# A Mamba block and a quantised feed-forward on one core: layer-norm statistics moved from VectorE to ScalarE, three more products per chunk on VectorE, pieces placed anew, and the last tile in column groups

## The reference, cut to what matters

```python
h = _layernorm(x) * (1 + ca) + sa
xc, z = split(h @ W_in.T, 2)                    # 1024 channels each
xc = silu(conv4(xc)); dlt, Bm, Cm = split(xc @ W_xproj.T)
delta = softplus(dlt @ W_dt.T + b_dt)
for t: state = exp(delta[t]*A) * state + delta[t]*xc[t]*Bm[t]     # 1024 x 16 states
       y[t] = sum_n state[:, n] * Cm[t, n]
x = x + ga * (((y + xc * D) * silu(z)) @ W_out.T)
h = _layernorm(x) * (1 + cb) + sb
g = silu(q(h) @ q(w_gate).T) * (q(h) @ q(w_up).T)     # 1408 wide, q: blocks of 16 to 4 bits
x = x + gb * (q(g) @ q(w_down).T)
```

## Time and profile before

| | |
|---|---|
| median of three runs | 5463.88 us (5456.84 to 5471.98) |
| the profiled execution | 5463.87 us, its span 5462.1 us |
| PE busy | 4869.5 us (89%) |
| DVE busy | 4934.1 us (90%) |
| POOL busy | 3984.4 us (73%) |
| ACT busy | 3061.0 us (56%) |

### The profile page before, as it was taken

The page is one execution under the profiler, slowest core; times in us unless marked ns, Lnnn a source line. Parts: engine busy times, 40 slices in busy tenths (PEclk is TensorE's granted clock), DMA queues, the critical chain, the costliest instruction groups (busy, mean ns, idle before and its releaser), DMA issues. The chain is left out here.

```text
span 5462.1 us, 76768 instructions
## 1 busy us (share of the span) xinstructions
PE 4869.5 (89%) x21996; PEld 3349.7 (61%) x21996; DVE 4934.1 (90%) x4312; ACT 3061.0 (56%) x6567; POOL 3984.4 (73%) x1960
## 2 busy tenths in 40 slices
PE   7589898898988989889898898976899999999999
PEld 3355555555555555555555555554788888888887
DVE  7899999999999999999999999999788888888887
ACT  2677777777777777777777777775211111111111
POOL 5899999999999999999999999999122222222221
PEclk9799999999999999999999999987999999999999
DMA  6455555555555555555555555555110101010100
GB/s 221 153 181 175 186 177 184 185 174 186 179 180 187 174 185 175 184 186 170 187 174 184 190 173 187 172 171 175 63 35 29 35 29 35 29 35 29 35 29 27
DMA packets 399478, 745.62 MB, mean 137 GB/s; under 512 B 44067, under 2 KB 44195, under 8 KB 398982
## 3 DMA queue, kind: packets, MB, share of 16 engines
q1 hardware_dynamic: 394758, 724.18, 40.5%
q0 software_dynamic: 4352, 17.30, 0.9%
HBM read 698.05 MB, written 43.26 MB: 136 GB/s over the span
## 5 line engine op out<-in xcount | busy, mean ns | idle before, releaser
L664 POOL TENSOR_TENSOR slot<-du,b_row 128x1024 f32<-128x1024 f32 x1024 | 2402.2, 2371 | 36.3 <-PE y_ps L1158 36.1
L1027 DVE TENSOR_TENSOR_SCAN decays<-decays,state,slot 128x1024 f32<-128x1024 f32 x608 | 1428.0, 2349 | 68.9 <-ACT slot L881 68.2
L872 ACT ACTIVATE decays<-delta,rate 128x512 f32<-128x512 f32 x2048 | 1327.0, 680 | 24.5 <-ACT state L859 2.8
L1158 PEld LDWEIGHTS y_ps<-ident,slot 128*128 128x128 f32 x8192 | 998.5, 148 | 322.9 <-issue 264.2
L1158 PE MATMUL y_ps<-ident,slot 128*128 128x128 f32 x8192 | 1088.8, 284 | 69.7 <-POOL slot L671 37.4
L1083 PE MATMUL work_ps<-h_t,win 128*128 128x512 f32 x2048 | 982.2, 624 | 114.7 <-ACT zs L750 92.4
L1512 POOL TENSOR_TENSOR hq<-hid,qinv 128x1408 f32<-128x1408 f32 x64 | 165.9, 2592 | 1227.2 <-DVE qinv L1538 1227.2
L671 POOL TENSOR_TENSOR slot<-slot,c_row 128x1024 f32<-128x1024 f32 x416 | 986.3, 2371 | 57.3 <-ACT state L859 57.3
L1027 DVE TENSOR_TENSOR_SCAN slot<-decays,state,slot 128x1024 f32<-128x1024 f32 x416 | 974.3, 2342 | 49.2 <-ACT slot L881 49.1
L1033 DVE TENSOR_TENSOR slot<-decays,c_row 128x1024 f32<-128x1024 f32 x608 | 742.7, 1221 | 47.7 <-DVE decays L1027 2.8
L1469 ACT ACTIVATE act_gate<-gate_ps 128x512 f32<-128x512 f32 (+1 forms) x192 | 108.2, 563 | 1125.8 <-PE gate_ps L1628 602.7
(11 more groups left out here) (234 smaller groups left out, 7560.6 us busy)
## 6 DMA issues: line engine op xcount, KB each, us to landing
b_row<-b_c_rows SPq DMA_DIRECT2D x1024, 256.0 KB, 3.8
c_row<-b_c_rows SPq DMA_DIRECT2D x1024, 256.0 KB, 3.7
win<-in_w_in SPq DMA_DIRECT2D x256, 256.0 KB, 4.2
xt<-in_x SPq DMA_DIRECT2D x16, 1024.0 KB, 6.7
xr<-in_x SPq DMA_DIRECT2D x64, 256.0 KB, 4.7
x_after_mamba<-xr SPq DMA_DIRECT2D x64, 256.0 KB, 4.4
xa<-x_after_mamba SPq DMA_DIRECT2D x64, 256.0 KB, 2.8
xres<-x_after_mamba SPq DMA_DIRECT2D x64, 256.0 KB, 2.7
```

The source lines that it names most:

```text
L664: pool.tensor_tensor(slot[:, u % SLOTS, :, :], du[:, p % 2, :, :], two(b_row[:, u % BC_RING, :]), ALU.mult).then_inc(S["ub_ready"], 1)
L872: act.activation(decay[u % 2][:, i, :], delta[:, p % 2, i, :], ACT.Exp, scale=rate[:, 2 * p + i, n:n + 1]).then_inc(S["decay_ready"], 1)
L1027: dve.tensor_tensor_scan(d if u in DVE_C else h, d, h, state[:, 2 * p, n:n + 1], ALU.mult, ALU.add).then_inc(S["scan_done"], 1)
L1158: op = pe.matmul(y_ps[i][:, s, :], slot[:, u % SLOTS, i, s * P:(s + 1) * P], ident[:, :], is_transpose=True, start=False, stop=(n == N - 1 ...
```

## The change

Five things change together.

1. **Statistics on ACT.** `ln_stats`, `ln_mean` and `x1_stats` leave DVE. In the Mamba part ACT takes the sum of each tile by a Copy with `accum_out` and the sum of squares by a Square with the negative mean as bias; the polish on POOL shrinks from eight small operations to four.
2. **The second norm per tile.** In the feed-forward part ACT makes the statistics of tile t+2 at the head of `body(t)`: two passes over 512 columns, eight operations on one column, and two table loads. The arrays of statistics, bn_aggr over 60 tiles and the chains on DVE go away. The first two tiles' statistics stand among the weight groups.
3. **C products.** `DVE_C` has 41 units instead of 38.
4. **Pieces placed anew** in all five tables and in `BANK`; `PART_J` is 6 instead of 5, so that the late projections have 12 steps instead of 16.
5. **The last tile in column groups.** The hidden values of tile 63 are quantised group by group (512, 512, 384 columns) on DVE alone (`end_quantise`), turned group by group (`end_turn`) and projected into another bank (`end_down`).

```diff
-PART_J = 5
-PART_AT = (51, 53, 55, 60)
+PART_J = 6
+PART_AT = (54, 56, 58, 60)
 PE_STEPS (end of a chunk)
-    53: [("x", 0, 1), ("z", 1, 1)], 54: [("d", 0, 1)], 55: [("d", 1, 1)], 58: [("z", 2, 1)], 59: [("y", 5, 0)],
-    62: [("d", 2, 1)], 63: [("z", 3, 1)],
+    50: [("c", 7, 1), ("y", 4, 0)], 51: [("z", 0, 1), ("y", 5, 0)], 53: [("x", 0, 1)], 54: [("d", 0, 1), ("z", 1, 1)],
+    56: [("d", 1, 1), ("z", 2, 1)], 57: [("z", 3, 1)], 58: [("d", 2, 1)], 60: [("z", 4, 1)],
 ACT_STEPS (start of a chunk)
+    0: [("sp_ln", 2, 0), ("xd", 0, 0)], 1: [("ln_sum", 0, 1), ("ln_sum", 1, 1), ("z_out", 4, 0)],
+    2: [("y_out", 6, -1)], 3: [("y_out", 7, -1)], 4: [("ln_sum", 2, 1), ("sp_exp", 3, 0)],
+    5: [("sp_ln", 3, 0), ("z_out", 5, 0)], 6: [("ln_sum", 3, 1)],
+    7: [("ln_square", 0, 1), ("ln_square", 1, 1), ("xd", 3, 0)], 8: [("ln_square", 2, 1), ("ln_square", 3, 1)],
+    9: [("xd", 2, 0)], 10: [("seed", 0, 1), ("z_out", 6, 0), ("residual", 0, -1)], 11: [("lead", 1, 0)],
 DVE_STEPS
-    (0, 0): [("sp_sum", 2, 0)], (0, 1): [("ln_stats", 0, 1)], (3, 1): [("ln_stats", 1, 1), ("sp_diff", 2, 0)],
-    (4, 0): [("ln_stats", 2, 1), ("ln_stats", 3, 1)], (5, 0): [("ln_mean", 0, 1)], (5, 1): [("sp_out", 2, 0)],
-    (6, 0): [("gate", 6, -1)], (8, 0): [("gate", 7, -1)], (9, 0): [("sp_sum", 3, 0)], (10, 1): [("sp_diff", 3, 0)],
-    (11, 0): [("sp_out", 3, 0)], (15, 1): [("sp_sum", 4, 0)], (17, 0): [("sp_diff", 4, 0)],
-    (17, 1): [("sp_out", 4, 0)], (18, 1): [("sp_sum", 5, 0)], (19, 0): [("sp_diff", 5, 0)],
-    (20, 0): [("sp_out", 5, 0)], (21, 0): [("x1_stats", 0, -1)], (29, 0): [("gate", 0, 0)], (30, 1): [("gate", 1, 0)],
-    (31, 0): [("x1_stats", 1, -1)], (34, 1): [("sp_sum", 6, 0)], (36, 0): [("sp_diff", 6, 0)],
-    (36, 1): [("sp_out", 6, 0)], (37, 0): [("gate", 2, 0)], (43, 1): [("sp_sum", 7, 0)], (44, 0): [("sp_diff", 7, 0)],
-    (44, 1): [("sp_out", 7, 0)], (46, 1): [("x1_stats", 3, -1)], (48, 1): [("gate", 3, 0)], (50, 0): [("gate", 4, 0)],
-    (52, 1): [("x1_stats", 2, -1)], (55, 0): [("x_low", 0, 1)], (57, 1): [("sp_sum", 0, 1)],
-    (58, 0): [("sp_diff", 0, 1)], (58, 1): [("sp_out", 0, 1)], (59, 1): [("sp_sum", 1, 1)],
-    (60, 0): [("sp_diff", 1, 1)], (61, 1): [("sp_out", 1, 1)], (63, 0): [("gate", 5, 0)],
+    (0, 0): [("sp_diff", 2, 0)], (0, 1): [("sp_out", 2, 0)], (3, 0): [("gate", 6, -1)], (4, 0): [("sp_sum", 3, 0)],
+    (5, 1): [("sp_diff", 3, 0), ("gate", 7, -1)], (6, 1): [("sp_out", 3, 0)], (15, 1): [("sp_sum", 4, 0)],
+    (16, 1): [("sp_diff", 4, 0)], (17, 1): [("sp_out", 4, 0)], (18, 1): [("sp_sum", 5, 0)],
+    (19, 0): [("sp_diff", 5, 0)], (20, 0): [("sp_out", 5, 0)], (21, 1): [("gate", 0, 0)], (31, 0): [("sp_sum", 6, 0)],
+    (32, 0): [("sp_diff", 6, 0)], (32, 1): [("sp_out", 6, 0)], (33, 1): [("gate", 1, 0)], (37, 1): [("gate", 2, 0)],
+    (39, 1): [("sp_sum", 7, 0)], (41, 0): [("sp_diff", 7, 0)], (42, 1): [("sp_out", 7, 0)], (49, 0): [("gate", 3, 0)],
+    (51, 1): [("gate", 4, 0)], (53, 0): [("gate", 5, 0)], (56, 0): [("x_low", 0, 1)], (57, 1): [("sp_sum", 0, 1)],
+    (58, 0): [("sp_diff", 0, 1)], (58, 1): [("sp_out", 0, 1)], (60, 0): [("sp_sum", 1, 1)],
+    (61, 0): [("sp_diff", 1, 1)], (61, 1): [("sp_out", 1, 1)], (62, 1): [("sp_sum", 2, 1)],
 POOL_STEPS
-    9: [("newton", 0, 1)], 13: [("du", 1, 0)], 16: [("lead_mul", 1, 0)], 22: [("du", 2, 0)], 23: [("lead_mul", 2, 0)],
-    46: [("du", 3, 0)], 47: [("lead_mul", 3, 0)], 63: [("du", 0, 1), ("lead_mul", 0, 1)],
+    0: [("lead_mul", 0, 0)], 10: [("du", 1, 0)], 11: [("newton", 0, 1)], 16: [("lead_mul", 1, 0)], 23: [("du", 2, 0)],
+    26: [("lead_mul", 2, 0)], 44: [("du", 3, 0)], 47: [("lead_mul", 3, 0)], 63: [("du", 0, 1)],
 DVE_C = (
-    0, 2, 4, 6, 7, 9, 11, 12, 13, 14, 16, 18, 20, 21, 23, 25, 26, 28, 30, 32, 33, 35, 37, 39, 40, 42, 44, 45, 47, 49,
-    51, 52, 54, 56, 58, 59, 61, 63,
+    0, 1, 4, 6, 7, 8, 9, 10, 11, 13, 14, 16, 18, 20, 21, 22, 24, 25, 27, 28, 31, 32, 34, 35, 36, 39, 40, 42, 43, 44,
+    45, 47, 48, 50, 52, 53, 56, 57, 60, 61, 62,
 )
...
+                    def ln_sum(s, c):
+                        act.activation(xt[:, s, :], xt[:, s, :], ACT.Copy, accum_out=ln_total[:, s:s + 1])
+                    def ln_square(s, c):
+                        act.activation(ln_junk[:, :], xt[:, s, :], ACT.Square, bias=ln_neg[:, s:s + 1], accum_out=ln_sq[:, s:s + 1])
...
+                    def body(t):                                  # ACT, feed-forward part
                         if exists_tile(t.shift(2)) and not is_first(t.shift(2)):
+                            act.preload_act_table_set("natural_log_exp_and_others")
+                            sum_row(t.shift(2))
+                            square_row(t.shift(2))
+                            seed_row(t.shift(2))                  # ends with the load of silu_and_others
+                            polish_row(t.shift(2))
                             norm(t.shift(2))
...
+                    weights_scalar(act, {2: lambda: sum_row(early), 3: lambda: square_row(early), 4: lambda: seed_row(early),
+                                         5: lambda: polish_row(early), 6: lambda: norm(early), 8: lambda: sum_row(late_one),
...
                         if exists_tile(t):                        # PE, feed-forward part
                             up_gate(t, 2)
+                        if closes(t):
+                            end_turn(0)
+                        if closes(before):
+                            end_down()
```

299 lines of the change are left out of this document (171 added, 128 removed), and 27 rows, old and new, of tables (BANK, PE_STEPS).

## The result

The changed kernel takes 5406.93 us (median of three, 5401.53 to 5410.99) against 5463.88: ratio 0.9894, 95% interval 0.9868 to 0.992. The forecast was 5386, range 5335 to 5440, so the measured time lies inside the range, 21 us above the forecast. To see why, the terms of the sum have to be laid beside the two profiled executions (spans 5462.1 and 5405.0 us, 57.1 apart). The marks are starts or ends of single instructions in the two traces.

A forecast was written before the change was run, and what follows sets the result against it. DVE and POOL together were taken to bound the Mamba part, PE the feed-forward part. From 5463.9: -66 (fifteen periods), -3 (last chunk), 0 (start), 0 (feed-forward), +1 (first tile), -9.4 (last tile) gives 5386.5 us; range 5335 to 5440.

The forecast's parts named there:

- A: Mamba chunks: the forecast itself, DVE's and POOL's stretches both set the period; 223.4 us per chunk, 5386 us; chance 0.60.
- B: Mamba chunks: DVE's waits stay because ACT and PE are late, only 0.7 us per chunk won; 5445 us; chance 0.15.
- C: Mamba chunks: DVE and POOL nearly stop waiting for each other; 220 us per chunk, 5331 us; chance 0.12.
- D: Mamba chunks: ACT's eight new passes hold scans in units 1 to 8, slower than before; 5501 us; chance 0.07.
- E: The change does nothing in the chunks, only the end of the kernel gains; 5455 us; chance 0.06.
- the rest of the period, 3.8 us, stays in this account: Mamba chunks: the 3.8 us between the tally's 224.0 and the traced 227.8, waits neither DVE nor POOL makes, assumed unchanged.
- Order around the chunk's end: Mamba chunk's end: `lead_mul` no longer delays POOL's first product, PE's third `d` piece comes earlier; nothing counted beyond the tally.
- Last chunk: Last Mamba chunk: no statistics of a next one, only the extra products, between -7 and +4; -3 us taken.
- Start: Program start: first statistics take two ACT passes, but DVE idles 7.00 us for a weight load; 0 taken, up to +2.
- First tile: First feed-forward tile: 4.9 us more ACT statistics, tile 2's load about 3 us earlier, Silu table loaded; +1 us taken.
- Feed-forward part: Steady feed-forward tiles: ACT's 6.2 us of new statistics hidden under 9.2 us cover, 14.7 before DVE notices; cost 0.
- Last tile: Last feed-forward tile: quantised, turned and projected in column groups, last add earlier by 8 to 10; -9.4 us taken.

The follow-up runs named there:

- e6: Changed kernel with its 12 middle chunks written out and three C products moved from DVE back to POOL (38 on DVE); 5442.49 us, ratio 0.996.
- e5: Changed kernel with its 12 middle chunks written out and ACT's eight statistics passes per chunk over 8 columns instead of 512; 5378.82 us, ratio 0.9843.
- e1: Changed kernel with both y_out on ACT behind unit 4 instead of units 2 and 3, and related pieces later; 5481.32 us, ratio 1.0034.
- e3: Kernel before the change with the 12 middle Mamba chunks written out instead of looped; 5449.95 us, ratio 0.9973.
- e8: Changed kernel with one table switch instead of four for the first two feed-forward tiles' statistics; 5404.61 us, ratio 0.9887.
- e12: Changed kernel with the edits of e8, e9 and no loops, second tile's statistics four groups later, each tile's statistics and norm behind its first Silu; 5356.99 us.
- e9: e7 plus POOL's two row products on tile 2 placed behind its product on tile 0's hidden values; 5398.71 us, ratio 0.9887.
- e7: Changed kernel with feed-forward tile 2's statistics moved from tile 0's head to behind its gate group 0 and tile 1's head; 5401.93 us, ratio 0.9887.
- e10: Changed kernel with each feed-forward tile's sum taken nine times instead of once on ACT; 5393.94 us, ratio 0.9876.
- e4: Changed kernel with the last tile done whole width as in the kernel before, without column groups; 5413.22 us, ratio 0.9914.
- e2: Changed kernel with the 12 middle Mamba chunks written out instead of looped; 5375.07 us, ratio 0.9844.

## Why the prediction was right, and where it was not

- **The total**: the terms' errors are +2.9, +12.0, +1.8, +6.4, +2.1, -5.1 and +0.4, and the sum is 20 us off and not 26 because one of them, which was not foreseen, has the other sign. That is luck.
- **The mechanism of the chunks** (A, both engines' stretches set the period): right. e6 shows that the period follows POOL's load at 38 products and that the gain comes with the three that move; e5 shows ACT's passes to be free; the loads per chunk were right to 1.5 us. By the period of 224.3, B (227), C (220), D (over 230) and E (227.8) are out. What B starts from, scans that wait as before, did come true; without the jumps C's 220 is nearly reached (221.9).
- **Its size**, -4.4 per chunk: right without jumps (-4.6), mis-sized with them (-3.6 over 15 periods, -54.0 instead of -66). The step that failed is "the rest of the period, 3.8 us, stays in this account". A third of that rest, (3188.1 - 3170.7)/14 = 1.2 us per chunk, was the loop's jump, and the change raised it to 2.4 (from 3.5 to 6.8 us per jump, with the spread said above). Most of what a jump costs the changed kernel is the wait of unit 3, 23.2 us over five jumps, and e1 takes it away by moving `y_out` back: it had come one or two units closer to PE's standstill. "Order around the chunk's end: I count nothing" left out this place. The rows were there: in the kernel before, PE's idle time "for issue" at every second chunk's start.
- **The scans' waits** were to fall to 3 us or less. They stayed at 6.6; without jumps they are (37.8 + 22.1)/14 = 4.3.
- **Last chunk**, -3: -1.2. The prediction gives it the extra products alone. But the kernel before has four `x1_stats` on DVE in this chunk as well (the result of chunk 14), and they go too. Even so the chunk wins less than the others; no run took it apart.
- **Start**, 0: +2.9 in this trace, above its upper bound of 2, but most of that is spread. The first scan comes at 167.7 to 171.9 us in the twelve traces with the new statistics (in e5 with fewer columns), 169.2 in the middle, and at 168.4 and 168.9 in the two traces of the kernel before and e3. So the term itself was about right.
- **First tile**, +1, from 0 to +4: the other failed step. Measured +7.4 to the first Silu and +2.1 behind it. "Four late steps fewer let that load leave about 3 us earlier" was wrong by 6 us: against the last scan it leaves 3.2 us later. Four late steps fewer did not bring it forward. By the trace it was held up by ACT's statistics among the weight copies and DVE's quantisation behind them. e8 shows that it was not the table loads, and in e12, with the second tile's statistics four groups later, the first Silu comes 48.4 us behind the last scan instead of e9's 51.6. e7 and e9 show the other half, the 5.2 us in front of the norm.
- **Feed-forward part**, 0: -5.1 over 61 tiles. e10 uses some 12.5 us of ACT's cover and the tile does not grow, so the cover does not end at 9.2; its end at 14.7 was not reached by a run. A tile is 24.76 us before and 24.68 after, not the 24.5 of the prediction, whose window of 245 us holds 9.9 tiles. What failed is "nothing but PE's own work can shorten it". PE's 2.4 us of idle time in 245 was a wait for DVE, whose chain is 2 us longer by POOL's row products beside it. This held in the kernel before too: its two operations at L209 and L212 take 1962 and 1862 ns there, and 895 and 895 in the changed kernel, where the products lie one operation further on; that operation and the next pay instead, 2598 and 2595 ns for 1625. The four together are 0.09 us shorter than before, which is 5.6 us over 61 tiles (an estimate) and accounts for the -5.1.
- **Last tile**, -9.4: -9.0 by the traces, 9.2 by e4, 3.7 of it by the granted clock.
- **The chances**: the range 5335 to 5440 was said to hold A, C and most of B, but C's own time, 5331, and B's, 5445, both lie outside it, so it held less than the 0.8 that was written. D has 0.07 in one place and 0.06 in another.
- **Table loads**: in the earlier trace rows a load takes 1.28 us and the next activation follows at once; the three loads shown under e7 start 1.5 to 1.6 us apart with an activation of 0.29 and one of 0.20 us between them. So no drain shows beside them, and the sum without one was the right one. Two more of them than counted stand before the second tile's statistics, since Ln and Exp are loaded one by one where no set is chosen ahead.

## What to carry to other kernels

In this kernel, work taken off a full engine won nothing (e6) until other work moved onto it: price the pair, not the move. Before a piece is moved, look at who is queued behind it on its own engine and on the helper's, and at the idle time "for issue" of the producer it would now meet: a loop's jump stands at a fixed place, and a table of pieces decides who pays and how much (2.9 to 3.5 us per jump before, 4.8 to 7.0 after). If an engine that should be the bound shows a few tenths of wait per tile on a partner, look whether the partner sets the pace, and compare the partner's operations with their own shortest duration.

## What the runs showed of the hardware

- Behind each jump back, with a body two chunks long (12322 matmuls over 14 chunks, so about 1760), PE stands still for 3.5 to 6.4 us in the kernel before and 5.2 to 7.1 in the changed one, in one stop or two of over 1 us. At the one shown the instruction queue moves 8 packets in 25 us, and 1 where nothing jumps. Written out (e2, e3), 12 chunks run without any such stop.
- A DVE operation with two inputs in SBUF takes 2.60 us instead of 1.62 (1408 columns), and 1.65 instead of 0.69 (512 columns), beside a POOL product; a DVE operation of one input on 1408 columns takes 1.96 instead of 0.90. With more work on ACT in front of that product (e10) the kernel was 13 us faster.
